# One operation on VectorE adds each output to the accumulator, values 0 and 1 are split first in step 4, and values load in quarters: an attention and FFN kernel in fp32

## The reference

```python
xn = _layernorm(x, axis=-1)                     # x: 1 x 2048 x 256
# attention, 16 heads of 128
k = jnp.einsum('ihd,bpd->biph', W_K, xn)
q = jnp.einsum('ihd,bpd->biph', W_Q, xn)
v = jnp.einsum('ihd,bpd->biph', W_V, xn)
scores = jnp.einsum('biph,biqh->biqp', k, q)
masked = scores * mask - 1e10 * (1.0 - mask)    # causal
attn = softmax(masked / sqrt(128), axis=-1)
z = jnp.einsum('biqp,biph->biqh', attn, v)
out = jnp.einsum('df,bqf->bqd', W_O, z_flat)
# feed-forward
hidden = fwht(silu(xn @ W1.T) * (xn @ W3.T))    # 1024 wide, Walsh-Hadamard
result = x + out + hidden @ W2.T
```

## Time and profile before

| | |
|---|---|
| median of 3 runs | 1411.65 us (1407.65, 1411.65, 1414.73) |
| the profiled execution | 1413.05 us |
| its span, first to last instruction | 1411.0 us |
| mean granted clock of TensorE | 0.984 |
| PE busy | 1342.5 us, 95% |
| PEld busy | 1198.1 us, 85% |
| DVE busy | 938.8 us, 67% |
| ACT busy | 950.2 us, 67% |
| POOL busy | 961.2 us, 68% |
| DMA | 330.72 MB, mean 234 GB/s |

### The profile page before, as it was taken

How to read it: one execution, slowest core, us unless ns; L and a number is a source line. 1 busy time by engine, 2 the same in 40 slices (tenths; PEclk the granted TensorE clock), 3 DMA queues, 4 the chain that set the end, 5 groups by cost and what they waited for, 6 DMA issues and landing times.

```text
span 1411.0 us, 26546 instructions
## 1 busy us (share of the span) xinstructions
PE 1342.5 (95%) x8138; PEld 1198.1 (85%) x8138; DVE 938.8 (67%) x2131; ACT 950.2 (67%) x1926; POOL 961.2 (68%) x634
## 2 busy tenths in 40 slices
PE   6999999999999999999999999999999999999987
PEld 5788888788888888888888888888888888888876
DVE  6544200767767777777777777787777777777763
ACT  4332344677768777778776877787778777877774
POOL 6111000277869787879787978797879787978794
PEclk9999999999999999999999999999999999999999
DMA  4200166797888889888888898888898889898883
GB/s 151 71 1 0 37 193 189 205 293 252 263 271 258 287 259 288 259 285 259 281 258 270 272 283 269 286 266 287 259 286 264 287 262 290 256 287 263 278 252 98
DMA packets 275741, 330.72 MB, mean 234 GB/s; under 512 B 62576, under 2 KB 248048, under 8 KB 271344
## 3 DMA queue, kind: packets, MB, share of 16 engines
q1 hardware_dynamic: 275696, 330.19, 74.6%
HBM read 170.85 MB, written 159.25 MB: 234 GB/s over the span
## 4 chain that ended last, share of the span: by engine, by line
POOL 41%; issue 29%; PE 17%; DMA 4%; SPq 3%; DVE 3%; ACT 2%; POOLq 1%; ACTq 0%; DVEq 0%
POOL pt_lo L462 28%; POOL acc L453 9%; PE ps L970 6%; PE ps L971 6%; PE ps L972 6%; SPq L353 3%; DMA scratch<-raw 3%; POOL v_lo L467 3%; DMA pt_lo<-scratch 1%; POOL wqk_lo L442 1%; DVE raw L902 1%; ACT raw L655 1%; POOLq L461 1%; DVE had L892 0%; DVE pt_lo L913 0%
## 5 line engine op out<-in xcount | busy, mean ns | idle before, releaser
L462 POOL TENSOR_TENSOR pt_lo<-pt_lo,pt_hi 128x896 fp32r<-128x896 f32 (+2 forms) x378 | 651.8, 1756 | 140.1 <-ACT pt_hi L662 140.0
L655 ACT ACTIVATE raw<-ps,had 128x1024 f32<-128x1024 f32 (+7 forms) x384 | 329.4, 867 | 163.6 <-DVE had L895 133.7
L902 DVE STREAM_TRANSPOSE raw<-raw 128x2048 f32<-128x2048 f32 (+3 forms) x252 | 317.0, 1292 | 105.5 <-ACT raw L655 103.2
L970 PE MATMUL ps<-pt_hi,v_hi 128*128 128x256 f32 (+1 forms) x1152 | 327.1, 284 | 35.1 <-POOL v_lo L467 27.4
L971 PE MATMUL ps<-pt_lo,v_hi 128*128 128x256 f32 (+1 forms) x1152 | 333.2, 289 | 0.0
L972 PE MATMUL ps<-pt_hi,v_lo 128*128 128x256 f32 (+1 forms) x1152 | 331.0, 287 | 0.0
L662 ACT CAST pt_hi<-pt_lo 128x896 fp32r<-128x896 f32 (+2 forms) x378 | 284.5, 818 | 35.4 <-DMA pt_lo<-scratch 35.1
L892 DVE TENSOR_REDUCE had<-ps 128x1 f32<-128x1024 f32 (+1 forms) x256 | 237.4, 947 | 46.9 <-PE ps L972 46.7
L970 PEld LDWEIGHTS ps<-pt_hi,v_hi 128*128 128x128 f32 x1152 | 223.2, 194 | 46.0 <-POOL v_lo L467 30.6
L970 PE MATMUL ps<-k_hi,q_hi 128*128 128x512 f32 (+3 forms) x640 | 235.7, 368 | 7.0 <-DVE k_lo L866 5.9
L971 PE MATMUL ps<-k_lo,q_hi 128*128 128x512 f32 (+3 forms) x640 | 233.8, 365 | 0.0
(11 more groups left out here) (113 smaller groups left out, 2222.6 us busy)
## 6 DMA issues: line engine op xcount, KB each, us to landing
v_next<-all_values SPq DMA_DIRECT2D x16, 1024.0 KB, 5.4
scratch<-raw SPq DMA_DIRECT2D x64, 256.0 KB, 5.6
pt_lo<-scratch SPq DMA_DIRECT2D x16, 1024.0 KB, 5.4
scratch<-raw SPq DMA_DIRECT2D x64, 240.0 KB, 5.0
pt_lo<-scratch SPq DMA_DIRECT2D x16, 960.0 KB, 5.9
scratch<-raw SPq DMA_DIRECT2D x64, 224.0 KB, 5.2
pt_lo<-scratch SPq DMA_DIRECT2D x16, 896.0 KB, 4.7
scratch<-raw SPq DMA_DIRECT2D x64, 208.0 KB, 4.7
```

Of the source, the lines that this page charges most:

```text
L462: pool.tensor_tensor(lo, lo.bitcast(F32), hi.bitcast(F32), ALU.subtract).then_inc(pt_lo_done, 1)
L655: act.activation(to, scores, ACT.Exp, bias=neg_max[:, j:j + 1], accum_out=row_part[:, j, e % 2:e % 2 + 1]).then_inc(exped, 1)
L902: dve.transpose(v, v).then_inc(blocked, 1)
L970: pe.matmul(dst, a[0], b[0], start=start, stop=False, skip_group_check=True)
```

## The change

ACT's `output` and POOL's `add` are gone, and with them the buffer `share` and the semaphore `shared`. DVE has an `output` instead: two `scalar_tensor_tensor` of 128x256, each multiplies half of the sum's bank in PSUM by the reciprocal and adds `acc`, into `acc`. For the big sums (2, 4, 6, 0) it stands first in DVE's steps 0, 2, 4, 6, for the small sums (3, 5, 7, 1) in the same steps behind both transposes. TensorE waits for a bank on `out_added`, which DVE now gives.

Values 0 and 1: ACT makes `v_hi` of both at the start of step 4, ahead of the exponentials; POOL makes `v_lo` of both first in step 4. The values come in four DMAs of 256 KB with a semaphore each: quarters 3 and 2 of the next head in SP's step 6, quarter 0 in step 7, quarter 1 in step 0.

On ACT, K slice 2 moves in step 7 from behind the three casts `p_to_hi` to ahead of them. In the last head `z_hi` of sum 3 is made in step 7 and not in the next step 0, and the first cast of that step stands behind it.

```diff
+    V_NEXT = {6: (3, 2), 7: (0,)}
 ...
-        v_moved = sem("v_moved")
+        v_moved = [sem(f"v_moved{b}") for b in range(QUARTERS)]
 ...
-            def bring_v(h):
-                wait(sp, v_lo_done, QUARTERS * h)
-                sp.dma_start(v_next[:, :], all_values[h].rearrange("p i d -> p (i d)")).then_inc(v_moved, 16)
+            def bring_v(h, b):
+                wait(sp, v_lo_done, v_count(h - 1, b))
+                sp.dma_start(v_next[:, b * BANK:(b + 1) * BANK],
+                             all_values[h][:, b * PER_Q:(b + 1) * PER_Q, :].rearrange("p i d -> p (i d)")
+                             ).then_inc(v_moved[b], 16)
 ...
-                    if s == 5 and h + 1 < HEADS:
-                        bring_v(h + 1)
+                    for b in V_NEXT.get(s, ()) if h + 1 < HEADS else ():
+                        bring_v(h + 1, b)
+                    if s == 0 and h > 0:
+                        bring_v(h, V_ITEMS[-1])
 ...  POOL's period
-                    if (s - 1) in O_BIG or s == 0:
-                        back, z = O_BIG[(s - 1) % STEPS]
-                        if s == 0:
-                            back -= 1
-                        if not (first and back) and not (over and not back):
-                            add(h + back, z)
+                    for b in V_AT[4] if s == 4 and not over else []:
+                        v_to_lo(h, b)
 ...
-                    if s != 2 and s in O_SMALL or s == 3:
-                        back, z = O_SMALL[2 if s == 3 else s]
-                        if not (first and back) and not (over and not back):
-                            add(h + back, z)
 ...  ACT's period
-                    if s == 3 and not over:
-                        v_to_hi(h, 2)
+                    for b in V_AT[s] if s in (3, 4) and not over else []:
+                        v_to_hi(h, b)
 ...
                     if s >= 5 and more and not over:
-                        kq_to_hi(h, (("Q", 3), ("Q", 0), ("K", 1))[s - 5])
+                        for item in ([("Q", 3)], [("Q", 0)], [("K", 1), ("K", 2)])[s - 5]:
+                            kq_to_hi(h, item)
 ...
-                    if not (first and s < 2) and not over:
+                    if not (first and s < 2) and not over and not (s == 7 and not more):
                         p_to_hi(hh, ss, 0)
-                    if s in (1, 3, 5) and not absent(Z_SMALL[s][0]):
+                    if s in ((1, 3, 5) if more else Z_SMALL) and not absent(Z_SMALL[s][0]):
                         z_to_hi(h + Z_SMALL[s][0], Z_SMALL[s][1])
                     if not (first and s < 2) and not over:
+                        if s == 7 and not more:
+                            p_to_hi(hh, ss, 0)
                         p_to_hi(hh, ss, 1)
                         p_to_hi(hh, ss, 2)
-                    if s == 7 and more:
-                        kq_to_hi(h, ("K", 2))
 ...  DVE
+            def output(h, z):
+                c = Z_ORDER[z]
+                dve.wait_ge(rcp_done, z_count(h, z))
+                dve.wait_ge(wo_product, z_count(h, z))
+                wait(dve, out_added, z_count(h, z) - 1)
+                for t in range(2):
+                    j = 2 * c + t
+                    ins = dve.scalar_tensor_tensor(
+                        out=acc[:, j, :], in0=z_bank(z, t * D, (t + 1) * D), scalar=row_rcp[:, j:j + 1],
+                        in1=acc[:, j, :], op0=ALU.mult, op1=ALU.add)
+                ins.then_inc(out_added, 1)
 ...  DVE's period
                 for s in range(5 if over else STEPS):
+                    if (s - 1) in O_BIG or s == 0:
+                        back, z = O_BIG[(s - 1) % STEPS]
+                        if s == 0:
+                            back -= 1
+                        if not absent(back):
+                            output(h + back, z)
                     if s in O_SMALL and not absent(O_SMALL[s][0]):
                         z_to_lo(h + O_SMALL[s][0], O_SMALL[s][1])
 ...
                     if not over and not on_tensor(h, s):
                         transpose_blocks(h, s, 1)
+                    if s in O_SMALL and not absent(O_SMALL[s][0]):
+                        output(h + O_SMALL[s][0], O_SMALL[s][1])
```

More of the change, by code:

```diff
@@ L673, in z_to_hi @@
                 act.copy(z_hi[:, :], z_bank(z, 0, CHUNK_Q)).then_inc(z_hi_done, 1)
-            def output(h, z):
-                c = Z_ORDER[z]
-                act.wait_ge(rcp_done, z_count(h, z))
-                wait(act, out_added, z_count(h, z) - 2)
-                act.wait_ge(wo_product, z_count(h, z))
-                for t in range(2):
-                    j = 2 * c + t
-                    ins = act.activation(share[:, z % 2, t, :], z_bank(z, t * D, (t + 1) * D), ACT.Copy,
-                                         scale=row_rcp[:, j:j + 1])
-                ins.then_inc(shared, 1)
             def period(h, first=False, more=True, over=False):
@@ L690, in period @@
                 for s in range(5 if over else STEPS):
-                    if s == 0 and not absent(O_SMALL[s][0]):
+                    if s == 0 and not absent(O_SMALL[s][0]) and not over:
                         z_to_hi(h + O_SMALL[s][0], O_SMALL[s][1])
-                    if (s - 1) in O_BIG or s == 0:
-                        back, z = O_BIG[(s - 1) % STEPS]
-                        if s == 0:
-                            back -= 1
-                        if not absent(back):
-                            output(h + back, z)
-                    if s == 3 and not over:
-                        v_to_hi(h, 2)
+                    for b in V_AT[s] if s in (3, 4) and not over else []:
+                        v_to_hi(h, b)
                     if s in (1, 3) and not absent(O_BIG[s][0]):
@@ L714, in period @@
                         exponential(h, s, 2)
-                    if s in O_SMALL and not absent(O_SMALL[s][0]):
-                        output(h + O_SMALL[s][0], O_SMALL[s][1])
                     if s < 2 and not over:
@@ L726, in period @@
                     if s >= 5 and more and not over:
-                        kq_to_hi(h, (("Q", 3), ("Q", 0), ("K", 1))[s - 5])
-                    for b in [] if over or s == 3 else V_AT.get(s, []):
-                        v_to_hi(h, b)
+                        for item in ([("Q", 3)], [("Q", 0)], [("K", 1), ("K", 2)])[s - 5]:
+                            kq_to_hi(h, item)
+                    if s == 0 and not over:
+                        v_to_hi(h, V_ITEMS[0])
                     if first and s < 4:
@@ L1054, in project_kq @@
                 elif item == ("K", 0):
[L1055 removed]
+                    pe.wait_ge(out_added, z_count(h, 1))
                 else:
```

18 lines of the change are left out of this document (6 added, 12 removed).

## The result

| | before | after |
|---|---|---|
| median of 15 runs each, same chip | 1407.9 us (1402.18 to 1415.71) | 1415.79 us (1409.38 to 1419.64) |
| ratio | | 1.0043, 95% interval 1.0026 to 1.006 |
| profiled execution, its span | 1413.05, 1411.0 us | 1417.17, 1415.3 us |
| mean granted clock | 0.984 | 0.996 |

The forecast was 1406 us, 0.4% under the 1411.65 us shown before. The measured time lies in the range and within the 0.5% that was called no change, but on the other side of zero. The profiled execution of the kernel before, 1413.05 us, was 5 us slower than the median of its fifteen, so its rows show somewhat longer heads than a usual execution has; the changed kernel's, 1417.17 us, is 1.4 us over its median.

A forecast was written before the change was run, and what follows sets the result against it. TensorE bounds the kernel but for some 2.4 us a head, mostly waiting for v_lo. A head of 67.9 + 2.5 + 0.2 = 70.6 us against 70.9 gives -4 us, the end -1.3: 1406 us, range 1388 to 1430.

The forecast's parts named there:

- the quarters cost nothing: Value loads in four DMAs: SP's waits for stores hide the extra issues; nothing taken, 7.4 us a head from above.
- D: Rival: the DMA queue becomes the bound through the quarter loads, 4.9 us a head more, 1475 us; chance 0.03.
- the head to be beaten: Length of a head of the kernel before, read from its profiled execution: 70.9 us.
- the head goes by the moment at which v_lo is ready: TensorE's wait for POOL's v_lo in step 4, 1.1 to 2.3 us a head, sets the head and goes.
- Rival B: The new waits for DVE are smaller, 1.2 us a head in place of 2.5: 1388 us; chance 0.27.
- the wait for z_lo of sum 5: New TensorE wait on DVE, late behind the output pair for sum 4: 1.2 us a head.
- that for the exponential: New TensorE wait at the scores of step 3, for the bank read by step 2's first exponential: 0.9 us.
- The wait for z_lo of sum 3: New TensorE wait, since K slice 2 ahead of ACT's casts makes z_hi of sum 3 late: 0.4 us a head.
- the new operation: DVE's output operation on 128x256, two a pair: 0.7 us a pair taken, 0.83 us from above.
- the end: After the last product DVE's pair takes the place of ACT's two copies: 1.3 us less.
- C: Rival: TensorE's waits of steps 2 and 3 draw the low clock, 1.2 us a head: 1423 us; chance 0.20.
- E: Rival: step 1's probabilities come late, a v_lo wait of about 1.2 us stays beside the new ones: 1423 us; chance 0.05.

The follow-up runs named there:

- e7: Kernel before with only the four quarter loads, in the places and order of the change: 1418.8 us, ratio 1.0046.
- e3: Changed kernel with the values loaded again in one DMA of 1 MB in step 5: 1409.0 us, ratio 0.9991.
- e16: Changed kernel with all four quarter loads issued one behind another in step 5: 1420.6 us, ratio 1.0068.
- e14: Kernel before without the value loads of heads 1 to 15: 1384.6 us, ratio 0.9808.
- e15: Changed kernel without the value loads of heads 1 to 15: 1402.6 us, ratio 0.9952.
- e5: Kernel before with only values 0 and 1 split first in step 4, on ACT and POOL: 1413.3 us, ratio 1.0001.
- e13: Changed kernel with one 1 MB load, in step 6, and DVE's outputs of sums 3, 5 and 7 ahead of the transposes: 1406.7 us, ratio 0.9996.
- e10: Changed kernel with one 1 MB load in step 5 and DVE's outputs of sums 3, 5 and 7 ahead of the transposes: 1405.6 us, ratio 0.9982.
- e11: Kernel before with values 0 and 1 split first in step 4 and K slice 2 ahead of step 7's casts: 1406.3 us, ratio 0.9978.
- e12: Kernel before with only the outputs moved to DVE, one load and the old order otherwise: 1411.5 us, ratio 1.0016.
- e2: Changed kernel with DVE's outputs of sums 3, 5 and 7 ahead of the transposes of their step: 1412.8 us, ratio 1.0031.
- e17: Kernel before, values 0 and 1 split first, K slice 2 ahead of the casts, 1 MB load issued from ACT's queue: 1420.7 us, ratio 1.0047.

## Why the prediction was wrong

**Wrong: the quarters cost nothing.** This is the step that failed: of the value loads in quarters the prediction said "I take nothing for it". Its ground was that SP's waits for stores hide the issues and that the same megabyte in parts costs the transfers behind it less. Measured, they cost 0.46% on the kernel before (e7; the interval goes from 0.19 to 0.74) and 1.0043 / 0.9991, 0.52%, on the changed one (e3), some 0.7 us a head (71.23 against 70.54). It is far less than the upper bound of 7.4 us a head, and D's 1475 us was rightly given 0.03; of D's sign half came: ACT waited more for moved probabilities, but SP waited for DVE no less than before (29.8 us in heads 2 to 13, 22.1 before).

By which way they cost it is not shown. The prediction had priced one of the ways itself: "If that cover is gone they cost 1.3 us a head of SP's time". Added up from the trace, SP issues for 55.3 us of each head of the kernel before (heads 2 to 13; 64 stores at 0.72 us are most of it), waits 10.5 us for stores to land and only 1.8 us for DVE, where one head had been read as 2.5:

```profile
L353 SPq DMA_DIRECT2D scratch<-raw x1008: 303/498/2400, 258.4 to 1374.9; - x168
```

So SP is nearly full, and its issues are a rival to the transfers. They take 54.5 us a head in e3, 56.6 in e16 and 57.0 in the changed kernel; the quarters by themselves are 1.3 us of the difference. In e16 the issues grew while the loads of probabilities land as soon as in e3; in the changed kernel these loads also take 0.3 us longer. No run adds issues without packets. The rule of the Trainium skill that the prediction cited against the quarters (DMA: Bandwidth & Descriptors, section Bandwidth) leaned the right way, and the runs agree by half a per cent.

**What remains of the miss.** Against the kernel before the forecast was a ratio of 0.996, measured was 1.0043, and the quarters are 0.5% of these 0.8%. Without them e3 stands at 0.9991 (0.9967 to 1.0015) and not at 0.996. The term that was mis-sized here is the head to be beaten: 70.9 us came from an execution 5 us over the median, which is 0.3 us a head (an estimate, 5.15 us over 15 heads), as much as the gain that was forecast. And 1406 us started from a median of three, 3.75 us above the median of fifteen. That 1406 and 14 heads of 0.7 us make 1416 us, as measured, is therefore luck: from 1407.9 the same sum gives 1412.

**Wrong in part: what a head's gain could be.** The prediction said that "the head goes by the moment at which v_lo is ready". Taking that wait away did not shorten the head, so something else lies close behind it. Three limits lie within some 2 us:

- the order on the engines of the kernel before: 68.57 us (e14), with a wait for v_lo of 1.00 us still in it;
- DVE's outputs in series with ACT's exponentials: 70.43 us (e3, e15);
- the load of 1 MB a head, through SP's round of issue, landing and return: a mean of 70.25 us or more in every kernel that had it, whatever stood on the engines, though single heads go down to 68.4 us (e5). The 70.25 is e13's, from an execution 6 us under its median. That this round is what carries it is argued and not shown: e10 and e11 were not run without the load.

Taking the v_lo wait away alone gave nothing (e5), with the k_lo wait's remedy too 0.22% (e11). Rival B's 1388 us was not reached by fewer waits for DVE: in e10 the head stayed at 70.5 us.

**Right: the exchange of waits, and the head's size by luck.** Without the quarters the forecast's 70.6 us a head is e3's 70.54. The v_lo wait went; the wait for z_lo of sum 5 was 1.16 us for 1.2, that for the exponential 0.65 for 0.9. The wait for z_lo of sum 3, 0.4 forecast, was 0.15 us. In a head of e15, where no load disturbs it, all waits over 0.1 us are 2.1 us where 2.7 were summed, and TensorE needs 68.3 us by itself where 67.9 was taken: two errors that cancel. ACT's idle time ahead of K slice 2 was 2.82 us for 2.9:

```profile
1175.86 0.60 ACT L587 ACTIVATE k_hi<-ps 128x512 fp32r<-128x512 f32 x1 [2.82 <-PE ps L966]
1176.36 2.19 ACT L653 CAST pt_hi<-pt_lo 128x896 fp32r<-128x896 f32 x3
```

That the waits of 0.64 and 0.63 us in steps 2 and 3 are costs of the outputs, and not of the values' new place, is shown by e12, and that the small outputs' place makes part of them by e2 and e10 (step 2 from 7.97 to 7.2 us).

**A size off: the new operation.** Taken was 0.7 us a pair; the rows of the changed kernel give 465 ns for one and 0.88 us for a pair from start to end, just over the upper bound of 0.83:

```profile
L897 DVE SCALAR_TENSOR_TENSOR acc<-ps,had,acc 128x256 f32<-128x256 f32 x256 | 108.6, 465 | 6.2 <-PE ps L966 6.2
L878 DVE TENSOR_TENSOR z_lo<-ps,z_hi 128x256 fp32r<-128x256 f32 x128 | 53.8, 421 | 43.0 <-ACT z_hi L664 42.8
```

**Right, but given back: the end.** From the start of the last output's products to the end of the span the kernel before took 1411.0 - 1405.18 = 5.8 us, the changed one 4.5: the 1.3 us of the forecast. But the last head as a whole grew from 96.1 to 96.7 us. In it DVE's pair for one sum stands ahead of the next sum's z_lo, and TensorE waits 1.35 us for that in place of 0.98. That does not explain the growth: e12 and e15 have the same pair and the same wait, and their last heads take 94.2 and 94.1 us. The last heads of the kernels with this order at the end run from 94.1 to 97.7 us (e15, e3), and what makes the difference is open.

```profile
1409.50 0.88 DVE L897 SCALAR_TENSOR_TENSOR acc<-ps,had,acc 128x256 f32<-128x256 f32 x2 [2.81 <-PE ps L966]
1410.29 0.41 DVE L878 TENSOR_TENSOR z_lo<-ps,z_hi 128x256 fp32r<-128x256 f32 x1
1410.76 0.39 PE L964 MATMUL ps<-wo_hi,z_hi 128*128 128x256 f32 x1 [1.35 <-DVE z_lo L878]
```

**Rivals C and E** did not come about: the granted clock was 1.00 in heads 2 to 13, and no wait for v_lo was left.

**The sum by parts.** Outputs on DVE +0.16% (e12, interval from -0.01 to 0.33), the two moves of order about -0.2% (e12 to e3, and e11), quarters +0.5% (e7; e3 to the change): +0.4 to +0.5%, the measured 0.43%. Only the quarters' part is well clear of zero: e12's interval holds zero, and e11's ends 0.04% short of it.

**Open.** What of SP's round makes 1 MB cost some 2 us a head is not settled. The DMA engines' mean busy share hardly changes without the loads (0.87 to 0.86 in the kernel before), so they are not plainly full. SP's own time does change: without the loads it issues for 53.8 us a head in place of 55.3 and waits 9.2 us for stores in place of 10.5. Another step or another queue for the load gave nothing (e13, e17); shorter packets elsewhere were not tried. Nor is it shown whether the quarters cost by their packet count, by the number of DMAs or by SP's issues.

## What to carry to other kernels

When one wait is removed and the time stays, look at what the removal should have shortened step by step: here the gain of one step came back in another, which suggests a bound beside the engines. A run that leaves the suspected traffic out, on both kernels, told what the reliefs of waits had not. Add up the time of the engine that issues the DMAs too, since no busy share of the page counts it: here SP issued for 55 of 71 us. Before a forecast of 0.4% the row that it starts from must be a usual one: the profiled execution here was 0.4% slow. And a large transfer cut into parts with shorter rows is an edit with a price of its own, to be bounded by a run before it is taken as free.

## What the runs showed that was not expected

- Heads are regular to 0.03 us where the engines' order bounds them (e3, e12, e15, and e14 where nothing disturbs it) and vary by 2 to 6 us in the others (e10: 69.3 to 73.0 us). The spread of the periods may serve as a sign of which bound holds.
- The cut of 1 MB into four DMAs of 256 KB raised the packets by 6,912 and the time by 0.5%. A DMA of 256 KB of weights beside them took 5.3 us in place of 3.2, one of 128 KB that no longer stood behind the megabyte 2.4 in place of 5.2.
- SP takes 0.72 us on average to issue one store of the scratch (0.30 to 2.40 us), and 64 of them fill 46 us of a head of 70.8.
- A second queue did not shield the small stores: 192 KB landed in 7.4 us in place of 4.8 beside the megabyte, which took 8.0 in place of 5.3.
- `scalar_tensor_tensor` of 128x256 with one operand in PSUM, one in SBUF and a scalar per partition took 465 ns, 44 more than the subtraction with the same operands (421).
